# Decay product in two 32-row waves, the removal key summed in PSUM, 512-column products in halves, and the bonus product in front of the scores

## The chip, the cores and the metric

The kernel runs on one core of one Trainium2 chip. The metric is the device time of one execution in microseconds (us). Five engines work side by side, each through its own instruction list in order, and wait for one another through semaphores: TensorE (PE in the profile, with its weight loads as PEld), VectorE (DVE), ScalarE (ACT), GpSimd (POOL) and SyncE (SP, here only for issuing DMAs).

## What is computed

A block of a language model in float32: a recurrent attention layer over 8 sequences of 512 steps and 256 channels in 16 heads, then a mixture-of-experts layer. Only the attention layer's projections matter here; cut to these, the reference reads:

```python
xrg, xwa, xk, xv = x[None] + xx[None] * (lo + time_maa)
k = xk @ Wk.T
w2 = jnp.tanh(xwa @ decay_w1.T) @ decay_w2            # 64 hidden rows
w = -jax.nn.softplus(-(time_decay + w2)) - 0.5
kk = k + jnp.tanh(xk @ kkk_w1.T) @ kkk_w2             # 16 hidden rows
kk = kk / norm(kk per head)
a = sigmoid(time_aaaaa + xwa @ aaa_w1.T @ aaa_w2)
ma = sigmoid(time_misc_a + xwa @ ma_w1.T @ ma_w2)
k = k * ma + k * a * (1.0 - ma)
mk = sigmoid(time_misc_k + xk @ mk_w1.T @ mk_w2)
k = k * exp(w * mk);  b = -kk * a;  decay = exp(-exp(w))
# then per step: s = s*decay + (s a) b + v k, y = s r
rk = (r * k * time_faaaa).sum(-1)                     # the "bonus" per head
y = (group_norm(y) * ln_w + ln_b + rk * v) * g @ Wo.T
```

## The kernel before

**Blocks and bodies.** The 512 steps are cut into 16 blocks of 32 steps; a block has 8 x 32 = 256 columns (`COLS`), and the 256 channels lie in two halves of 128 partitions, so a whole tensor of a block is 128 x 512. A software pipeline runs over bodies n = -2 to 18. Body n makes the projections and scores of block n+1, turns keys and values of block n, solves, reads out and updates the state of block n-1, and projects, normalizes and stores block n-2, with the router's product of block n-3. The order inside a body is written out by hand for each engine in the functions `body(n)`. The mixture-of-experts layer follows after the last body and isn't touched.

**Banks.** Six PSUM banks are handed from job to job in a fixed order, the `Ring`. "z@1" is the job z in bank 1. A job's first product waits (`wait_empty`) until the steps listed for the bank's previous job in `freed` are done, and readers wait (`wait_full`) for its last product.

**The stretch in question on PE.** `hidden` makes the hidden rows (64 of the decay, then 16 each of four others, at the starts 64, 80, 96, 112). `square(.., "k", ..)` makes k in bank 3. `decay_a_kk` makes z (the decay's exponent) as one product over all 128 rows, then a and kk side by side, each over 32 rows; `ma_mk` makes ma and mk side by side. `router` (block n-3, 8 columns each) and `project_out` (block n-2) follow, then the first half of `solve`, `norms` (head sums of kk squared), the second half of `solve`, the products r and v with transposes of keys and values, `read_out`, `bonus`, `update`, `read_out`, and the `scores`.

**ACT and DVE.** ACT copies k out of its bank (`keep_k`, L1085), turns z into its biased copy and its sigmoid (`keep_z`, `sigma_of_z`, L1058), and applies the other sigmoids; the helper line of all biased halves is L1029. DVE adds kk and k (`sum_kk`, L1420), scans the decay (`sum_decays`, L1400, which waits for the sigmoid of z), forms the key gains (L1406, L1408), adds the tokens of block n-2 (`add_tokens`, L1546, which waits for `project_out`), and goes on to the masked keys (`mask_removal` L1476, `mask_keys` L1445) that `scores` waits for. Each fp32 product is two records in the trace. L576 is the line of the helper `fill`, L622 that of `from_hidden`, L718 `solve`, L662 `scores`, L594 `low_2` (the mixing of the next block but one), L1389 the first reader of `low_2` on DVE.

## Time and profile before

| | |
|---|---|
| median of 3 runs | 1076.15 us (1071.28 to 1077.69) |
| the profiled execution's own time | 1076.19 us |
| its span, first to last instruction | 1074.1 us |
| PE busy | 980.1 us (91%) |
| DVE busy | 768.0 us (71%) |
| ACT busy | 519.9 us (48%) |
| mean granted clock of PE, share of full speed | 0.951 |
| bodies with blocks in all stages | 39.2 to 46.9 us each |

PE's busy share is high, but PE is no proof of a bound by itself: its records overlap the waits of the others, and a body ends where the last of PE, DVE and ACT lets the next one go on. The granted clock has two levels, 1.0 (2.4 GHz) and 0.5 (1.2 GHz); a body whose mean is under 1.0 holds a stretch at the lower one.

### The profile page before, as it was taken

The numbers are of one execution on the slowest core, as the hardware profiler recorded it, in microseconds if no ns is written. First come the engines' busy times: TensorE is split into PE (matmuls) and PEld (weight loads), VectorE is DVE, ScalarE is ACT, GpSimd is POOL, SyncE is SP. The second block draws the span as 40 slices with busy tenths as digits, with TensorE's granted clock in tenths as the row PEclk, the third lists the DMA queues.
The fourth block names the chain that finished last, engine by engine and source line by source line (L and its number), as shares of the span: only waits on it lengthen the run. The fifth ranks groups of instructions, "written<-read, shape, count | busy, mean of one in ns | idle before, by whom it ended". The sixth has DMA issues, their size and how long they took to land.

```text
span 1074.1 us, 42156 instructions
## 1 busy us (share of the span) xinstructions
PE 980.1 (91%) x16652; PEld 801.8 (75%) x16653; DVE 768.0 (71%) x1793; ACT 519.9 (48%) x1081; POOL 613.1 (57%) x1135
## 2 busy tenths in 40 slices
PE   8898989999999989999999998679899999999995
PEld 5676777777777767777777776557899898989894
DVE  5766788889879778887688885266476666666663
ACT  4474576677677576676476783221122121212120
POOL 1088786788886787785867876810133333333321
PEclk9997999999999999998799998689999999999998
DMA  5113225225324225224143133746545445544430
GB/s 121 40 21 81 71 33 110 65 51 111 77 47 101 70 44 111 72 42 107 17 101 87 28 91 85 206 115 232 217 163 176 161 174 162 176 158 170 158 119 4
DMA packets 208894, 112.14 MB, mean 104 GB/s; under 512 B 172508, under 2 KB 192224, under 8 KB 208352
## 3 DMA queue, kind: packets, MB, share of 16 engines
q1 hardware_dynamic: 202352, 100.92, 35.0%
q0 software_dynamic: 3744, 8.40, 2.3%
q8 instruction: 121, 1.98, 0.8%
q10 hardware_dynamic: 2640, 0.54, 0.3%
q14 instruction: 37, 0.30, 0.1%
HBM read 85.57 MB, written 26.08 MB: 104 GB/s over the span
## 4 chain that ended last, share of the span: by engine, by line
PE 61%; DVE 14%; issue 8%; POOL 6%; DMA 5%; ACT 4%; DVEq 1%; SPq 1%; ACTq 0%; POOLq 0%
PE bank L576 16%; PE bank L970 12%; PE bank L983 9%; PE bank L662 6%; PE ry L983 4%; PE bank L718 3%; POOL arena L1914 3%; POOL arena L1911 3%; DVE bank L1389 2%; PE ry L692 2%; PE bank L594 1%; PE bank L622 1%; PE bank L950 1%; PE ry L698 1%; PE bank L740 1%
## 5 line engine op out<-in xcount | busy, mean ns | idle before, releaser
L576 PE MATMUL bank<-arena 128*128 128x256 f32 (+2 forms) x992 | 280.9, 422 | 22.4 <-DVE arena L1434 9.5
L1914 POOL TENSOR_TENSOR arena<-arena 128x30 f32<-128x30 f32 (+14 forms) x480 | 261.6, 545 | 37.6
L1911 POOL TENSOR_TENSOR arena<-arena 128x30 f32<-128x30 f32 (+14 forms) x480 | 250.5, 522 | 36.4
L576 PEld LDWEIGHTS bank<-arena 128*128 128x128 f32 x992 | 178.5, 203 | 67.9 <-issue 31.5
L970 PEld LDWEIGHTS bank<-arena 128*128 128x128 f32 x1248 | 146.8, 194 | 5.8 <-issue 3.0
L970 PE MATMUL bank<-arena 128*128 128x128 f32 x1248 | 147.5, 277 | 3.1 <-DVE arena L1820 2.5
L1498 DVE TENSOR_TENSOR arena<-bank,arena 128x512 f32<-128x512 f32 x128 | 79.5, 684 | 53.1 <-PE bank L662 53.1
L1302 ACT ACTIVATE arena<-arena 128x1 f32<-128x1 f32 x39 | 11.5, 294 | 178.6 <-DVE arena L1774 178.6
L983 PE MATMUL bank<-arena 128*128 x416 | 96.4, 385 | 0.1
L1945 POOL COPY arena<-arena 128x1 int32 (+1 forms) x39 | 7.1, 183 | 146.4 <-DVE arena L1838 146.4
L983 PEld LDWEIGHTS bank<-arena 128*128 128x128 f32 x416 | 76.9, 190 | 14.5 <-issue 4.9
L662 PE MATMUL bank<-arena 32*128 32x64 f32 x2048 | 68.9, 276 | 10.6 <-issue 6.4
L1939 POOL DMA_INDIRECT arena<-scr_x,arena x39 | 41.2, 1056 | 62.4 <-DVE arena L1756 31.4
L662 PEld LDWEIGHTS bank<-arena 32*128 32x128 f32 x2048 | 64.0, 189 | 14.9 <-issue 13.4
L1389 DVE SCALAR_TENSOR_TENSOR bank<-bank,arena 128x256 f32<-128x256 f32 x128 | 56.1, 484 | 22.2 <-PE bank L594 22.2
L670 PE MATMUL bank<-arena 128*128 128x128 f32 x432 | 62.5, 279 | 4.2 <-DVE arena L1511 1.6
L670 PEld LDWEIGHTS bank<-arena 128*128 128x128 f32 x432 | 52.1, 144 | 18.8 <-issue 12.4
L1904 POOL MEMSET arena<- 128x32 f32 x16 | 2.5, 157 | 111.2 <-DMA arena<-scr_n 111.2
L718 PEld LDWEIGHTS bank<-arena 32*64 32x64 f32 x2048 | 40.1, 157 | 34.6 <-issue 29.6
L1820 DVE TENSOR_SCALAR arena<-bank,arena 128x128 f32<-128x128 f32 x156 | 43.9, 345 | 24.6 <-issue 19.9
L1947 POOL DMA_INDIRECT out_dram<-arena x39 | 39.8, 1021 | 34.9 <-DVE arena L1804 20.8
L718 PE MATMUL bank<-arena 32*64 32x32 f32 x2048 | 43.8, 239 | 15.1 <-DMA arena<-scr_u 13.9
(173 smaller groups left out, 1757.7 us busy)
## 6 DMA issues: line engine op xcount, KB each, us to landing
arena<-in_W SPq DMA_DIRECT2D x47, 1024.0 KB, 5.1
scr_n<-arena SPq DMA_DIRECT2D x64, 128.0 KB, 3.0
arena<-scr_n SPq DMA_DIRECT2D x16, 512.0 KB, 3.7
scr_u<-arena SPq DMA_DIRECT2D x16, 512.0 KB, 4.5
arena<-scr_u SPq DMA_DIRECT2D x62, 128.0 KB, 2.9
arena<-in_xTp SPq DMA_DIRECT2D x32, 132.0 KB, 4.0
arena<-in_x SPq DMA_DIRECT2D x64, 64.0 KB, 2.7
scr_x<-arena SPq DMA_DIRECT2D x64, 64.0 KB, 1.8
```

What stands on the lines that cost most here:

```text
L576: mm = pe.matmul(ring.tile(m, name)[0:rows, to], lhsT, rhs, start=(i == 0), stop=(i == len(terms) - 1))
L662: mm = pe.matmul(ring.tile(m, f"sc{f}{p}")[:, b * 2 * TB:(b + 1) * 2 * TB], bkm[r, f * B + b, :], aq[m % 2][r, f * B + b].rearrange("p x t ...
L670: mm = pe.transpose(ring.tile(m, name)[:, i * P:(i + 1) * P], src, ident)
L718: mm[bank] = pe.matmul(ring.tile(m, f"x{bank}")[x_rows_of(e), at:at + 32], Ux[m % 2][r, g % 4, g // 4, e].rearrange("p h t -> p (h t)"), R ...
L970: mm = pe.matmul(hidT_ps[t // 4][:, (t % 4) * P:(t % 4 + 1) * P], W1[s][:, k, t * P:(t + 1) * P], xnT[:, k, :], start=(k == 0), stop=(k == ...
L983: mm = pe.matmul(y_ps[s][:, 0:D], hidT[s][:, t, :], W2f[:, bass.ds(e * (FT * D) + t * D, D)], start=(t == 0), stop=(t == FT - 1))
L1389: xm_ok.inc(m, f"{g}{h}", STT(out=part, in0=part, scalar=prm(f"maa{g}", h), in1=dx[:, h], op0=ALU.add, op1=ALU.mult))
L1498: score.inc(m, name, TT(sc[m % 2][:, f, p].rearrange("p k e x t -> p (k e) (x t)"), ring.tile(m, name)[:, :].rearrange("p (b n) -> p b n", ...
L1820: relu_dve.inc(str(t), nc.vector.tensor_scalar(hidT[s][:, t], hidT_ps[1][:, (t - 4) * P:(t - 3) * P], b1f[:, bass.ds(e * FT + t, 1)], 0.0, ...
L1911: inv_ok.inc(f"m{s}", TT(t, U[:, 0:s, s:s + 1].broadcast_to(shape), U[:, s:s + 1, s + 1:TB].broadcast_to(shape), ALU.mult))
L1914: inv_ok.inc(f"a{s}", TT(U[:, 0:s, s + 1:TB], U[:, 0:s, s + 1:TB], t, ALU.add))
L1939: nc.gpsimd.indirect_dma_start(out=xg[:, s], out_offset=None, in_=x_rows, in_offset=bass.IndirectOffsetOnAxis(ap=index, axis=0), bounds_ch ...
```

## The change

Five edits, all in the 16 bodies that have a block n+1 to project.

1. `decay_a_kk` now makes in one wave of three products, side by side, the first 32 hidden rows of z, all of a, and the 32 rows of kk; kk is added onto the product k that is still in bank 3, as the first product there starts the bank and the others don't. The wave waits for all three banks first; the bank of kk is free when `keep_k` has read it.
2. `decay_ma_mk` is a second wave with the other 32 rows of z, and ma and mk; z is complete after it. It stands behind `router`, and `logit` moves from bank 3 to bank 0.
3. DVE's `sum_kk` is gone. ACT copies the sum out of the bank instead (`keep_kk`) and squares it from the bank; ACT's order becomes a, logits, copy and square of kk, z.
4. `norms`, `centre_y` and `variance_y` each make two products of 256 columns instead of one of 512.
5. `bonus` moves behind the second `read_out`.

```diff
-        proj: "k z0 z1 sg a0 a1 ma0 ma1 abs sq sab mk0 mk1 ..."
-        comb: "kk scan t f k2 ..."
+        proj: "k a0 a1 kk sq z0 z1 sg ma0 ma1 abs sab mk0 mk1 ..."
+        comb: "scan t f k2 ..."
-        freed: "kk": [(comb, "kk")]
+        freed: "kk": [(proj, "sq")]
-        ... (1,"z@1 a@5 kk@3 ma@4 mk@2"), (-3,"logit@3"), (-2,"wo@0"), ...
+        ... (1,"a@5 kk@3"), (-3,"logit@0"), (1,"z@1 ma@4 mk@2"), (-2,"wo@0"), ...
             def decay_a_kk(m):
                 hid_act.wait(pe, m, "decay", "copy", "kkk")
-                from_hidden(m, [[("z", 2, slice(0, P), hid)]])
-                from_hidden(m, [[("a", 0, slice(64, 96), hid), ("kk", 0, slice(96, 128), kkh)]])
+                for name in ("z", "a", "kk"):
+                    ring.wait_empty(pe, m, name)
+                for h, to in both:
+                    mm_z = pe.matmul(ring.tile(m, "z")[:, to], w_out[0:32, 2, hs(h)], hid[0:32, :], start=(h == 0), stop=False,
+                                     skip_group_check=True)
+                    mm_a = pe.matmul(ring.tile(m, "a")[:, to], w_out[64:96, 0, hs(h)], hid[64:96, :], start=True, stop=True)
+                    mm_kk = pe.matmul(ring.tile(m, "kk")[:, to], w_out[96:128, 0, hs(h)], kkh[96:128, :], start=False, stop=True,
+                                      skip_group_check=True)
+                mm_z.then_inc(half_decay, 1)
...
+            def decay_ma_mk(m):
+                pe.wait_ge(half_decay, m + 1)
+                for name in ("ma", "mk"):
+                    ring.wait_empty(pe, m, name)
+                for h, to in both:
+                    mm_z = ... w_out[32:64, 2, hs(h)], hid[32:64, :], start=False, stop=True
+                    mm_ma, mm_mk = ... as before
             def norms(m):
-                fill(m, "ss", [(all_cols, [(head_sum, flat(nrm))])])
+                fill(m, "ss", [(to, [(head_sum, nrm[:, h])]) for h, to in both])
...
 PE body(n):
                 if has(n + 1):
-                    ma_mk(n + 1)
-                if -1 <= n <= 0:
-                    keep_busy(4, ry_bank[0])
-                if has(n - 3):
                     router(n - 3)
+                    decay_ma_mk(n + 1)
+                    keep_busy(4, ry_bank[0])   # n = -1, 0
...
-                    bonus(n + 1)               # between the two read_outs
+                    bonus(n + 1)               # behind the second
 ACT body(n):
-                    keep_z sigma_of_z keep_a keep_ma abs_of_z keep_logits(n - 3) square_kk sigma_of_abs keep_mk
+                    keep_a keep_logits(n - 3) keep_kk square_kk keep_z sigma_of_z keep_ma abs_of_z sigma_of_abs keep_mk
 DVE body(n):
-                    sum_kk(n + 1)
```

PE's list around the decay product, in a body that has all stages; the lines of the changed kernel are shifted, L622 becomes L621, L623, L624 (z, a, kk) and L635, L637, L638 (z, ma, mk), and L576 becomes L577. Before:

```order
L576 MATMUL bank<-arena 128x256 x6
L670 MATMUL bank<-arena 128x128 x4
L622 MATMUL bank<-arena 128x256 x10
L576 MATMUL bank<-arena 128x8 x4
L576 MATMUL bank<-arena 128x256 x4
L718 MATMUL bank<-arena 64x32 x32
L576 MATMUL bank<-arena 128x512
L718 MATMUL bank<-arena 64x32 x32
```

and now, from the second half of the first wave on:

```order
L621 MATMUL bank<-arena 128x256
L623 MATMUL bank<-arena 128x256
L624 MATMUL bank<-arena 128x256
L577 MATMUL bank<-arena 128x8 x4
L635 MATMUL bank<-arena 128x256
L637 MATMUL bank<-arena 128x256
L638 MATMUL bank<-arena 128x256
L635 MATMUL bank<-arena 128x256
L637 MATMUL bank<-arena 128x256
L638 MATMUL bank<-arena 128x256
L577 MATMUL bank<-arena 128x256 x4
L727 MATMUL bank<-arena 64x32 x32
```

The router's four products now stand between the two waves, and the last product of z behind them.

ACT's list over the same stretch, each with the semaphores that it waits for (proj, comb and the filled banks). Before, L1085 is the copy of k, L1150 the copy of turned keys, L1058 the sigmoid of z, L1212 the logits, L1097 the square:

```order
L1085 ACTIVATE arena<-bank 128x512 [waits filled3,comb]
L1150 ACTIVATE arena<-bank 128x512 [waits filled2,filled0]
L1029 ACTIVATE arena<-bank,arena 128x256 [waits filled1,comb]
L1029 ACTIVATE arena<-bank,arena 128x256
L1058 ACTIVATE bank<-arena 128x512 [waits proj]
L1029 ACTIVATE arena<-bank,arena 128x256 [waits filled5,comb]
L1029 ACTIVATE arena<-bank,arena 128x256
L1029 ACTIVATE bank<-bank,arena 128x256 [waits filled4]
L1029 ACTIVATE bank<-bank,arena 128x256
L1064 ACTIVATE arena<-arena 128x512 [waits proj,comb]
L1212 ACTIVATE arena<-bank 128x16 [waits filled3]
L1097 ACTIVATE arena<-arena 128x512 [waits comb,filled0]
```

and now, L1094 being the copy of k, L1226 the logits, L1111 and L1105 the copy and the square of kk, and L1067 the sigmoid of z:

```order
L1094 ACTIVATE arena<-bank 128x512 [waits filled3,comb]
L1164 ACTIVATE arena<-bank 128x512 [waits filled2,filled0]
L1038 ACTIVATE arena<-bank,arena 128x256 [waits filled5,comb]
L1038 ACTIVATE arena<-bank,arena 128x256
L1226 ACTIVATE arena<-bank 128x16 [waits filled0]
L1111 ACTIVATE arena<-bank 128x512 [waits filled3,comb]
L1105 ACTIVATE arena<-bank 128x512 [waits filled0]
L1038 ACTIVATE arena<-bank,arena 128x256 [waits filled1,comb]
L1038 ACTIVATE arena<-bank,arena 128x256
L1067 ACTIVATE bank<-arena 128x512 [waits proj]
L1038 ACTIVATE bank<-bank,arena 128x256 [waits filled4]
```

Five instructions now stand between the copy of the turned keys and the first reader of z, where there was none.

PE's list in front of the scores, before (L752 `read_out`, L740 `update`, L662 `scores`):

```order
L670 MATMUL bank<-arena 128x128 x12
L752 MATMUL ry<-arena 32x32 x32
L576 MATMUL bank<-arena 128x256 x2
L740 MATMUL bank<-arena 32x32 x32
L752 MATMUL ry<-arena 32x32 x32
L662 MATMUL bank<-arena 128x64 x32
```

and now:

```order
L679 MATMUL bank<-arena 128x128 x12
L761 MATMUL ry<-arena 32x32 x32
L749 MATMUL bank<-arena 32x32 x32
L761 MATMUL ry<-arena 32x32 x32
L577 MATMUL bank<-arena 128x256 x2
L671 MATMUL bank<-arena 128x64 x32
```

The bonus (the 128x256 x2) has moved past one `update` and one `read_out`.

## Rows read from the trace of the kernel before

**Rows 1.** The page: span, busy time by engine, granted clock in 40 slices

```profile
span 1074.1 us, 42156 instructions
...
PE 980.1 (91%) x16652; PEld 801.8 (75%) x16653; DVE 768.0 (71%) x1793; ACT 519.9 (48%) x1081; POOL 613.1 (57%) x1135
...
PEclk9997999999999999998799998689999999999998
```

**Rows 2.** Busy time by body, cut where DVE starts L1420

```profile
core 0: us, PE busy (x) PEld busy (x) DVE busy (x) ACT busy (x) POOL busy (x), PEclk, DMA share, GB/s
139.54:178.72 39.18, 35.13 (x899) 27.36 (x900) 33.41 (x62) 27.14 (x50) 29.39 (x56) 1.00 0.26 56
...
296.95:337.41 40.46, 38.02 (x912) 29.82 (x910) 33.67 (x63) 28.34 (x54) 29.36 (x56) 0.96 0.31 70
...
461.42:503.17 41.75, 38.22 (x910) 29.97 (x910) 33.57 (x63) 27.82 (x54) 29.09 (x55) 0.96 0.27 57
503.17:550.11 46.94, 44.72 (x914) 34.56 (x910) 33.71 (x63) 28.74 (x55) 33.85 (x66) 0.82 0.34 71
...
590.78:630.53 39.75, 36.68 (x914) 28.86 (x912) 32.37 (x59) 28.06 (x54) 32.89 (x64) 1.00 0.34 78
```

**Rows 3.** Who PE waited for, 110 to 630 us: us in total, times, longest

```profile
PE bank L576 <- DVE arena L1434: 7.4, 11, 1.2
PE bank L576 <- DVE arena L1420: 5.9, 9, 0.9
```

**Rows 4.** Who DVE waited for, 110 to 630 us

```profile
DVE bank L1389 <- PE bank L594: 16.3, 13, 3.0
DVE arena L1546 <- PE bank L576: 12.9, 11, 2.8
```

**Rows 5.** Timeline of PE, decay product to solve: start, us, line, count

```profile
334.59 2.96 PE L622 MATMUL bank<-arena 128*128 128x256 f32 x20
338.23 2.86 PE L576 MATMUL bank<-arena 128*128 128x8 f32 x16 [0.69 <-DVE arena L1420]
341.02 1.13 PE L718 MATMUL bank<-arena 32*64 32x32 f32 x64
```

**Rows 6.** Timeline of DVE over the same stretch

```profile
337.41 0.68 DVE L1420 TENSOR_TENSOR arena<-bank,arena 128x512 f32<-128x512 f32 x1
338.01 1.20 DVE L1400 TENSOR_TENSOR_SCAN arena<-arena,bank 128x512 f32<-128x512 f32 x1
...
339.83 0.70 DVE L1408 TENSOR_TENSOR bank<-bank,arena 128x512 f32<-128x512 f32 x1
341.20 0.69 DVE L1546 TENSOR_TENSOR arena<-bank,arena 128x512 f32<-128x512 f32 x1 [0.67 <-PE bank L576]
```

**Rows 7.** Timeline of ACT over the same stretch

```profile
334.41 0.60 ACT L1085 ACTIVATE arena<-bank 128x512 f32<-128x512 f32 x1 [0.95 <-PE bank L576]
...
335.72 0.84 ACT L1029 ACTIVATE arena<-bank,arena 128x256 f32<-128x256 f32 x2 [0.22 <-PE bank L622]
336.59 0.60 ACT L1058 ACTIVATE bank<-arena 128x512 f32<-128x512 f32 x1
...
339.30 0.18 ACT L1212 ACTIVATE arena<-bank 128x16 f32<-128x16 f32 x1
```

**Rows 8.** Timelines of PE and DVE in front of the scores

```profile
351.17 1.10 PE L576 MATMUL bank<-arena 128*128 128x256 f32 x4 [0.80 <-DVE arena L1434]
...
352.13 1.75 DVE L1445 TENSOR_TENSOR arena<-arena 128x512 f32<-128x512 f32 x2
...
354.03 0.73 PE L662 MATMUL bank<-arena 32*128 32x64 f32 x17
```

**Rows 9.** Timeline of PE: one product of 512 columns

```profile
322.79 1.12 PE L576 MATMUL bank<-arena 128*128 128x512 f32 x2
```

**Rows 10.** Busy time in two neighbouring stretches, columns as in Rows 2

```profile
313.70:316.80 3.10, 2.57 (x65) 2.39 (x66) 0.71 (x3) 1.34 (x2) 2.79 (x5) 1.00 0.00 0
316.80:320.20 3.40, 3.40 (x16) 2.22 (x19) 2.33 (x4) 0.94 (x3) 2.93 (x7) 0.50 0.02 5
```

More of the change, by code:

```diff
@@ L570, in _, with fill @@
         def _(pe):
-            def fill(m, name, parts, cols=slice(0, HALF * COLS), rows=P):
+            def fill(m, name, parts, cols=slice(0, HALF * COLS), rows=P, started_once=False):
                 ring.wait_empty(pe, m, name)
-                for to, terms in parts:
+                for j, (to, terms) in enumerate(parts):
                     for i, (lhsT, rhs) in enumerate(terms):
-                        mm = pe.matmul(ring.tile(m, name)[0:rows, to], lhsT, rhs, start=(i == 0), stop=(i == len(terms) - 1))
+                        mm = pe.matmul(ring.tile(m, name)[0:rows, to], lhsT, rhs, start=(i == 0 and not (started_once and j)),
+                                       stop=(i == len(terms) - 1), skip_group_check=started_once)
                 ring.fill(m, name, mm)
@@ L612, in hidden @@
                 ring.fill(m, "h", mm)
-            def from_hidden(m, parts):
-                for group in parts:
-                    for name, w, rows, x in group:
-                        ring.wait_empty(pe, m, name)
-                for group in parts:
-                    for h, to in both:
-                        for name, w, rows, x in group:
-                            mm = pe.matmul(ring.tile(m, name)[:, to], w_out[rows, w, hs(h)], x[rows, :], start=True, stop=True)
-                            if h == HALF - 1:
-                                ring.fill(m, name, mm)
@@ L637, in square @@
                 xm_ok.wait(pe, m, f"x{x}")
-                fill(m, name, [(to, [(w_sq[:, w, k, hs(h)], xm[x][:, k]) for k in range(HALF)]) for h, to in both])
+                fill(m, name, [(to, [(w_sq[:, w, k, hs(h)], xm[x][:, k]) for k in range(HALF)]) for h, to in both],
+                     started_once=(name == "k"))
             def gate_1(m):
@@ L880, in body @@
                     read_out(n - 1, 1 if n - 1 < last else 0)
+                if has(n + 1):
+                    bonus(n + 1)
+                if n == 0:
+                    keep_busy(7, ry_bank[0])
                 if n == last + 1:
@@ L1095, in square_kk, with keep_kk @@
                     ring.wait_full(act, m - 1, "ss")
-                comb.wait(act, m, "kk")
-                proj.inc(m, "sq", A(flat(nrm), flat(kk), ACT.Square))
+                proj.inc(m, "sq", A(flat(nrm), bank(m, "kk"), ACT.Square))
+            def keep_kk(m):
+                if m:
+                    comb.wait(act, m - 1, "kkn")
+                ring.wait_full(act, m, "kk")
+                proj.inc(m, "kk", A(flat(kk), bank(m, "kk"), ACT.Copy))
             def keep_gate(m):
@@ L1415, in key_exponent @@
                                      op0=ALU.add, op1=ALU.mult))
-            def sum_kk(m):
-                ring.wait_full(dve, m, "kk")
-                proj.wait(dve, m, "k")
-                comb.inc(m, "kk", TT(flat(kk), ring.tile(m, "kk")[:, :], flat(kt), ALU.add))
             def gain_keys(m):
-                comb.wait(dve, m, "f", "kk")
+                comb.wait(dve, m, "f")
                 comb.inc(m, "k2", TT(flat(kt), flat(kt), ring.tile(m, "ma")[:, :], ALU.mult))
@@ L1642, in body @@
                     mix_stage(n + 2)
-                if has(n + 1):
-                    sum_kk(n + 1)
                 if n == last + 2:
```

40 lines of the change are left out of this document (24 added, 16 removed), and 2 rows, old and new, of the table ring.

## The prediction

> **What bounds the kernel now.** The page comes first: PE has a record running 91% of the span [rows 1], so a change on PE looks worth its full size. Then the windows by body, to see what a body costs and what moves it. The chains of waits of PE and DVE follow, and last the timelines of one body, to see who waits for whom in what order. The fourteen bodies between 139 and 631 us cut at DVE's L1420 tell two things: the clean ones at granted clock 1.00 take 39.2 to 39.75 us (five of them), those with one stretch at half clock 40.5 to 41.9 (six), one with more 46.9 [rows 2]. A slow stretch so costs about 41.15 - 39.4 = 1.8 us (mean of the six against mean of the clean).
>
> The loop that closes a body runs through both engines in turn. DVE waits for PE's `low_2`: 16.3 us in 13 waits [rows 4]. From then on DVE works through its list to the masked keys (L1445), and PE starts the scores 0.15 us behind their end, 354.03 against 352.13 + 1.75 = 353.88 [rows 8]. Then PE alone leads, through scores, state read-out and the next `low_2`. In DVE's part one wait of note is left, that for `project_out`, 0.67 us in this body, 12.9 us in 11 waits in all [rows 4, 6]. So whatever comes before the scores counts only as far as it moves DVE's list; PE's own 0.7 to 0.8 us waits there [rows 5, 8] are slack, not price.
>
> **The decay in two waves.** On PE, the old group has twelve rounds one behind the other (four for z, four for a and kk together, four for ma and mk together: each product is two records) in 2.96 us with its drain [rows 5], some 0.24 us a round. The new one has eight, which saves about 0.96 us of PE, and the 0.69 us wait of the router goes too, since its bank no longer hangs on `sum_kk`. But the result z comes later, and this is what DVE needs.
> - The first wave waits for all three banks, kk's being free when the copy of k ends: 334.41 + 0.60 = 335.01 [rows 7]. The old z had started at 334.59 [rows 5]. So start at about 335.08, that is 0.5 us lost, with nothing beside it on PE.
> - A wave of four rounds takes 0.95 us to the next instruction and 1.13 us to its reader on ACT (334.59 to 335.72, [rows 5, 7]). The first is handed over at 336.2, the router starts at 336.0.
> - The router: from 338.23 to the solve at 341.02 are 2.79 us, of which eight records of 256 columns take 8 x 0.23 = 1.84, so it takes 0.95 [rows 5]. The second wave then runs from 337.0, and z is complete for ACT at 338.1.
> - ACT meanwhile does a (336.2 to 337.05), the logits (0.18) when the router is through at 337.15, the copy and the square of kk (0.60 each, as the copy of k, which overlap by 0.1), to about 338.4 [rows 7]. The copy and sigmoid of z took from 335.72 to 337.19 = 1.47 us [rows 7]. Starting at 338.3 they end at 339.8.
> - DVE's scan waits for that sigmoid. It started at 338.01 with no wait, because `sum_kk` (0.68) lay in front of it [rows 6]. Now it starts at 339.8: 1.8 us later, though DVE has one instruction less. The 0.6 us that DVE gains by that is spent waiting.
> - Behind it, L1546 would come at 341.20 + 1.8 without its old wait of 0.67 [rows 6]: **1.1 us later**. `project_out` is through by 340.1 (337.95 + 1.84 and its drain), so it no longer covers anything. DVE has no other wait to absorb 1.1 us before the keys, so the scores start 1.1 us later, and this goes round in every body.
>
> PE's other steps don't turn this. `solve` takes bank 1 after z, so it waits for the scan's end (339.8 + 1.2 = 341.0, where it stood before); `norms` takes bank 0 after `project_out`, so it waits for L1546's end, 343.0. PE idles some 0.5 + 1.1 + 1.0 there; the saved 0.96 us is spent in these waits. ACT's further steps move by as much as the scan, up to 1.8 us at most, and DVE meets the logarithm that it needs (L1412) about when it is ready.
>
> **Over the run.** Six bodies like the one shown: 6 x 1.1 = 6.6. The first full one, where L1546 had no wait: 1.8. Of the 12.9 us of waits for `project_out` [rows 4], 12.9 - 6 x 0.67 = 8.9 are left for five more bodies; four in which PE was slow exactly there have 1.7 to 2.8 each (longest in [rows 4]), which could swallow all of 1.8, so 0 to 1.1 each, taken at the middle, 2.2. The last two have what is left of it, some 0.4 each: 2 x 1.4 = 2.8. The first three have no tokens to add and nothing to cover z: 5.4, and two of them have two filler products between the waves, 0.8 each: 1.6. Sum 20.4 us, with a clock as before.
>
> **The clock.** The granted clock was 0.50 from 316.8 to 320.2, behind a stretch of small 32-row products and waits in which PE was busy 2.57 of 3.10 us at clock 1.00 [rows 10]. The change makes another such place: waits of 0.5, 1.1 and 1.0 us around 32-row waves, the router and the half solves, between about 334.6 and 343. Two of the five clean bodies falling to half clock there would cost 2 x 1.8 = 3.6. Bounds: no slow stretch at all in the bodies, 7 x 1.8 + 5.8 = -18 us; one in every clean body and a second in some of the others, +15. I take +3.6, near the rows' own frequency. The Trainium skill, TensorE: Matmul & The Clock Gate (Part 1, HAM oscillation), lays the fall to idle gaps between bursts and asks to keep PE busy. By that rule alone the waits of about 1 us would cost nothing here and the sum stays at 20.4; rows 10 show a fall behind a stretch without one long gap, so I don't rely on it.
>
> **The halves.** A product of 512 columns took 1.12 us, two of 256 took 1.10 [rows 8, 9]. So nothing; the bounds are -0.1 and +0.1 us for each of three, and only `centre_y` lies where PE leads, so at most 16 x 0.1 = 1.6 us either way. The Trainium skill speaks against this edit: in the same page, Part 3 (What overlaps and what doesn't), a weight load overlaps with a running product only when their row groups differ. By that, the two more loads of 128 rows in each pair would lie open, and at the page's figure of 128 columns in some 0.11 us a load that would be an estimated 3 x 2 x 0.11 = 0.6 us a body on PE. The equal 1.12 and 1.10 us contradict it, and the sum goes by them.
>
> **The bonus.** Its wait for L1434 (7.4 us in 11 waits [rows 3]) goes, 0.80 us in this body. But `update` and `read_out` behind it then run earlier up to a wait of the same length for the keys, which end 353.88 whether PE waits once or twice [rows 8]. The product itself, 1.1 us, fits in that wait: PE comes to the bonus about 1.1 us behind its old pace, near 352.9, and to the scores at 353.95, while the keys are ready at 355.0. Price 0; were that cover gone, nothing would be added either, since the product ran before the scores already.
>
> **Rivals.**
> - *PE is the bound, and the change takes 0.96 off it* (faster). For it speaks the 91% [rows 1] and the waits for `project_out` [rows 4]. It needs z to reach DVE by 337.4; then `sum_kk` (0.6) and L1546's wait (0.67) go, 1.27 us in some 12 bodies: 1076.2 - 15 = **1061 us**. Against it the place of the second wave.
> - *The clock holds up better*: the dense bonus right before the scores ends the slow stretches behind them, about five in the bodies, so 20.4 - 5 x 1.8 = 11 us: **1087 us**.
> - *The waits hide z everywhere*: PE is late in most bodies as in the four with 1.7 to 2.8 us of cover, so half of the 20.4 goes or more: **1083 us**.
> - *The clock falls in every body* (slower still): the new waits are followed by half clock from `project_out` on, PE comes late to the scores as well: 20.4 + 15: **1112 us**.
>
> **How the numbers follow.** The profiled execution took 1076.19 us, the median is 1076.15, so its sum stands for both: 1076.2 + 20.4 + 3.6 = 1100.2, or **1100 us**. Chances: this forecast 0.44, the worse clock 0.20, the better clock 0.14, the hidden z 0.12, PE as the bound 0.10. The range leaves out the fastest rival and the far end of the worse clock: 1080 to 1116. About 1% (10.8 us) is what a measurement of this kernel can tell from no change. Slower by over 1% (above 1087): 0.44 + 0.20 + about half of the two middle rivals = 0.76. Within 1%: 0.14. Faster: 0.10.
>
> **What would show it.** Right: in the profile after, DVE sits idle some 2 us in front of the scan with ACT's sigmoid of z as the releaser, and no longer in front of L1546; PE waits for the scan before the solve and for the keys before the scores; clean bodies take 40.4 to 40.8 us; the two-wave group takes about 1.9 us in all; the halves take 1.1 us. Wrong: a scan that starts as soon as DVE is there, or clean bodies under 39.2 us, would say that z is not late; bodies over 41.5 with clocks of 0.9 and less that the clock, not the wait, sets the time.

## The result, and the profile after

The changed kernel takes 1122.56 us (median of 4 runs, 1117.18 to 1126.95), against 1076.92 before: a ratio of 1.044, 95% interval 1.038 to 1.049. Six more runs beside a later experiment gave 1121.29 us and 1.043 (1.038 to 1.049). The direction was forecast, the size (1100) was not: the time lies over the range. The ratios here leave out, on both sides, runs over 1.5% above a kernel's fastest; the medians are of all runs.

The page of the profiled execution (1119.93 us), lines as in [rows 1]:

```profile
span 1117.9 us, 42460 instructions
...
PE 987.2 (88%) x16812; PEld 826.9 (74%) x16813; DVE 757.5 (68%) x1777; ACT 530.0 (47%) x1097; POOL 611.1 (55%) x1135
...
PEclk9998989899988899799998898777999999999998
```

The busy times hardly changed: DVE 10 us less, ACT 10 us more, PE 7 us more (a record made at half clock takes longer, so PE's busy time rises with it). So the 44 us are waits and clock. Busy time in three stretches, cut at the scans of blocks 3 and 15, with the same cut of the kernel before behind it:

```profile
core 0: us, PE busy (x) PEld busy (x) DVE busy (x) ACT busy (x) POOL busy (x), PEclk, DMA share, GB/s
0.00:140.71 140.71, 118.03 (x1828) 92.39 (x1829) 91.02 (x166) 79.48 (x142) 74.76 (x144) 0.96 0.33 70
140.71:673.65 532.94, 470.75 (x11040) 381.33 (x11040) 395.98 (x717) 346.52 (x649) 384.09 (x731) 0.92 0.31 67
673.65:1117.90 444.25, 398.46 (x3946) 353.15 (x3944) 270.54 (x895) 104.05 (x308) 152.24 (x262) 0.94 0.46 151
```

```profile
140.15:631.13 490.98, 455.15 (x10909) 355.56 (x10907) 403.96 (x730) 337.36 (x633) 386.14 (x732) 0.96 0.34 73
```

Twelve full bodies hold 532.94 - 490.98 = 42.0 of the 43.8 us; the head has +0.6, the tail +1.3. Half-clock time in them, from the mean PEclk as 2 x (1 - clock) x time, rose from about 38 to 85 us. It isn't so much that the clock fell more often, 12 times instead of 8, as that it stayed down longer: seven of the eight stretches of before lasted 3.4 us and one 13.7, ten of the twelve after lasted 6.8 to 10.2. One of them began 1.1 us behind the end of the wait in front of the norms, which is the second line here:

```profile
275.06 1.13 PE L727 MATMUL bank<-arena 32*64 32x32 f32 x64 [1.01 <-DVE arena L1416]
277.05 1.10 PE L577 MATMUL bank<-arena 128*128 128x256 f32 x4 [0.86 <-DVE arena L1557]
```

```profile
278.18:285.01 6.83, 6.83 (x78) 5.86 (x79) 5.53 (x11) 3.00 (x7) 6.12 (x10) 0.50 0.01 2
```

Two of the twelve bodies ran at 1.00, and some were far from it (compare [rows 2]):

```profile
232.01:273.78 41.77, 36.20 (x921) 29.43 (x920) 33.10 (x60) 28.83 (x55) 31.37 (x60) 1.00 0.35 74
501.01:542.23 41.22, 36.11 (x922) 29.30 (x920) 32.84 (x61) 28.94 (x55) 29.52 (x56) 1.00 0.34 69
315.76:364.22 48.46, 42.10 (x922) 34.12 (x920) 33.06 (x61) 28.89 (x55) 32.78 (x63) 0.86 0.29 64
451.44:501.01 49.57, 43.70 (x922) 35.36 (x920) 33.43 (x60) 28.82 (x55) 35.71 (x69) 0.83 0.32 69
```

I cut every body of both traces at the same instructions, by the starts and ends of the instructions (mean us; clean means clock 1.00 throughout, in brackets how many bodies):

| part of the loop | before, clean (5) | after, clean (2) | before, all 12 | after, all 12 |
|---|---|---|---|---|
| scan to end of masked keys (DVE) | 15.94 | 14.97 | 16.68 | 16.17 |
| masked keys to scores (PE starts) | 0.32 | 0.84 | 0.50 | 1.87 |
| scores to next `low_2` (PE) | 10.60 | 10.97 | 11.05 | 11.31 |
| `low_2` to the copy of k | 9.25 | 9.11 | 9.27 | 9.44 |
| start of the copy of k to end of z's sigmoid | 2.78 | 5.49 | 2.78 | 5.51 |
| sigmoid to scan | 0.54 | 0.10 | 0.63 | 0.10 |
| body | 39.43 | 41.49 | 40.92 | 44.41 |

The two clean bodies are 2.06 us longer than those of before, where 40.4 to 40.8 us in all were forecast. The timelines of ACT just in front of a clean body's first scan, and of DVE in that body, answer to [rows 6, 7]; the sigmoid of z is L1067, the scan L1416, the tokens L1557:

```profile
226.21 0.60 ACT L1094 ACTIVATE arena<-bank 128x512 f32<-128x512 f32 x1 [0.97 <-PE bank L577]
...
228.19 0.84 ACT L1038 ACTIVATE arena<-bank,arena 128x256 f32<-128x256 f32 x2 [0.89 <-PE bank L623]
229.12 0.18 ACT L1226 ACTIVATE arena<-bank 128x16 f32<-128x16 f32 x1
229.47 0.60 ACT L1111 ACTIVATE arena<-bank 128x512 f32<-128x512 f32 x1 [0.16 <-issue]
...
230.44 0.84 ACT L1038 ACTIVATE arena<-bank,arena 128x256 f32<-128x256 f32 x2
231.31 0.60 ACT L1067 ACTIVATE bank<-arena 128x512 f32<-128x512 f32 x1
```

```profile
232.01 1.22 DVE L1416 TENSOR_TENSOR_SCAN arena<-arena,bank 128x512 f32<-128x512 f32 x1 [4.08 <-ACT bank L1067]
...
234.46 0.68 DVE L1557 TENSOR_TENSOR arena<-bank,arena 128x512 f32<-128x512 f32 x1
...
244.05 1.28 DVE L1487 TENSOR_TENSOR arena<-bank,arena 128x512 f32<-128x512 f32 x2
245.25 1.73 DVE L1456 TENSOR_TENSOR arena<-arena 128x512 f32<-128x512 f32 x2
```

z's sigmoid ends 5.7 us behind the start of k's copy here (5.49 or 5.50 in the other eleven), and DVE waits for it in every body; the wait in front of the tokens is gone. That was forecast. PE in the same body:

```profile
233.29 1.14 PE L727 MATMUL bank<-arena 32*64 32x32 f32 x64 [1.21 <-DVE arena L1416]
235.28 1.10 PE L577 MATMUL bank<-arena 128*128 128x256 f32 x4 [0.86 <-DVE arena L1557]
...
242.78 0.76 PE L761 MATMUL ry<-arena 128*32 128x32 f32 x64
245.48 0.76 PE L749 MATMUL bank<-arena 128*32 128x32 f32 x64 [1.94 <-DVE arena L1487]
246.08 0.76 PE L761 MATMUL ry<-arena 128*32 128x32 f32 x64
246.76 1.13 PE L577 MATMUL bank<-arena 128*128 128x256 f32 x4
247.82 2.01 PE L671 MATMUL bank<-arena 32*128 32x64 f32 x64
```

The two waves take 1.06 and 1.07 us in front of this body, 2.1 in all where 1.9 were forecast. The waits in front of the solve and of the norms are those forecast too (1.1 and 1.0). The third was not: `update` (L749) waits 1.94 us for L1487, the masked removal keys. Bank 0 goes from the squared norms, which L1487 reads last, to the state update (`freed["ss"]` names the step bm1). PE has 13.8 us of this wait in the twelve bodies. Behind it now stand the update, a read-out and the bonus, and only then the scores: they start at 247.82, 0.84 us after the masked keys are done (245.25 + 1.73 = 246.98). In the kernel before, the bonus ran before that wait and the gap was 0.15 us [rows 8].

### The profile page after: what moved, and what is told of

Its sections match the earlier page's. It is cut to its first block, busy times and chain, and to the rows that moved or that the text cites. A ratio compares the mean times of both kernels' runs of the same rounds, so it can differ in the third digit from the quotient of the medians.

```text
span 1117.9 us, 42460 instructions
## 1 busy us (share of the span) xinstructions
PE 987.2 (88%) x16812; PEld 826.9 (74%) x16813; DVE 757.5 (68%) x1777; ACT 530.0 (47%) x1097; POOL 611.1 (55%) x1135
## 4 chain that ended last, share of the span: by engine, by line
PE 63%; DVE 11%; issue 8%; ACT 6%; POOL 6%; DMA 5%; SPq 1%; DVEq 1%; ACTq 0%; POOLq 0%
PE bank L577 17%; PE bank L979 11%; PE bank L992 9%; PE bank L671 6%; PE ry L992 4%; POOL arena L1923 3%; POOL arena L1920 3%; PE bank L727 3%; PE ry L701 2%; PE bank L679 2%; PE ry L707 2%; PE bank L749 1%; PE bank L596 1%; PE bank L612 1%; PE bank L959 1%
## 5 line engine op out<-in xcount | busy, mean ns | idle before, releaser
L577 PE MATMUL bank<-arena 128*128 128x256 f32 (+1 forms) x1088 | 294.8, 413 | 17.3 <-DVE arena L1557 9.7
L577 PEld LDWEIGHTS bank<-arena 128*128 128x128 f32 x1088 | 206.7, 210 | 70.0 <-issue 30.2
L979 PEld LDWEIGHTS bank<-arena 128*128 128x128 f32 x1248 | 145.3, 192 | 5.6 <-issue 2.9
L992 PEld LDWEIGHTS bank<-arena 128*128 128x128 f32 x416 | 77.1, 190 | 14.3 <-issue 4.9
L671 PEld LDWEIGHTS bank<-arena 32*128 32x128 f32 x2048 | 67.2, 199 | 15.9 <-issue 14.0
L671 PE MATMUL bank<-arena 32*128 32x64 f32 x2048 | 72.2, 287 | 7.3 <-issue 3.5
L727 PEld LDWEIGHTS bank<-arena 32*64 32x64 f32 x2048 | 43.9, 170 | 44.7 <-issue 18.8
L727 PE MATMUL bank<-arena 32*64 32x32 f32 x2048 | 47.8, 250 | 31.5 <-DMA arena<-scr_u 17.4
L679 PEld LDWEIGHTS bank<-arena 128*128 128x128 f32 x432 | 53.8, 147 | 14.5 <-issue 7.2
L1956 POOL DMA_INDIRECT out_dram<-arena x39 | 39.7, 1018 | 34.9 <-DVE arena L1813 20.8
L1829 DVE TENSOR_SCALAR arena<-bank,arena 128x128 f32<-128x128 f32 x156 | 43.9, 345 | 21.8 <-issue 18.1
```

Of the source, the lines that this page charges most:

```text
L577: mm = pe.matmul(ring.tile(m, name)[0:rows, to], lhsT, rhs, start=(i == 0 and not (started_once and j)), stop=(i == len(terms) - 1), skip_ ...
L671: mm = pe.matmul(ring.tile(m, f"sc{f}{p}")[:, b * 2 * TB:(b + 1) * 2 * TB], bkm[r, f * B + b, :], aq[m % 2][r, f * B + b].rearrange("p x t ...
L679: mm = pe.transpose(ring.tile(m, name)[:, i * P:(i + 1) * P], src, ident)
L727: mm[bank] = pe.matmul(ring.tile(m, f"x{bank}")[x_rows_of(e), at:at + 32], Ux[m % 2][r, g % 4, g // 4, e].rearrange("p h t -> p (h t)"), R ...
L979: mm = pe.matmul(hidT_ps[t // 4][:, (t % 4) * P:(t % 4 + 1) * P], W1[s][:, k, t * P:(t + 1) * P], xnT[:, k, :], start=(k == 0), stop=(k == ...
L992: mm = pe.matmul(y_ps[s][:, 0:D], hidT[s][:, t, :], W2f[:, bass.ds(e * (FT * D) + t * D, D)], start=(t == 0), stop=(t == FT - 1))
```

## The experiments

All ratios are against the kernel before, measured beside it on the same chip. "Bodies" is the time of the same twelve bodies in one profiled execution, with the half-clock time in them. These two vary from execution to execution of one program (the two of the changed kernel differ by 7 us), and some of the profiled executions are far from their kernel's median: `u_zearly` is 13 us above it, `b_kksum` 13, `b_halves` 12, `b_repeat` 7 and `u_repeat` 5 us below; the others are within 4.

| kernel | median us (runs) | ratio, 95% interval | bodies us | half clock us |
|---|---|---|---|---|
| before, beside each group of runs | 1073 to 1078 | | 491 | 38 |
| changed | 1122.6 (4), 1121.3 (6) | 1.044 (1.038-1.049), 1.043 (1.038-1.049) | 533, 526 | 85, 85 |
| `u_bonus` | 1109.8 (4) | 1.031 (1.022-1.039) | 524 | 82 |
| `u_whole`, `_again`, `_third` | 1112.3 (4), 1111.4 (6), 1111.9 (6) | 1.027 (1.018-1.036), 1.032 (1.024-1.039), 1.034 (1.030-1.039) | 526, 525, 529 | 104, 82, 96 |
| `u_zdense` | 1097.0 (4) | 1.018 (1.007-1.028) | 519 | 61 |
| `u_zdense_bonus` | 1090.9 (4) | 1.014 (1.005-1.023) | 507 | 41 |
| `u_zdense_bonus_whole` | 1086.3 (4) | 1.012 (1.004-1.021) | 503 | 44 |
| `u_repeat` | 1109.7 (4) | 1.038 (1.030-1.046) | 517 | 34 |
| `u_zearly` | 1141.7 (4) | 1.058 (1.049-1.066) | 565 | 150 |
| `u_zearly_repeat` | 1152.1 (4) | 1.075 (1.065-1.085) | 557 | 82 |
| `u_zearly2` | 1112.6 (4) | 1.036 (1.027-1.044) | 524 | 65 |
| `u_zearly2_bonus` | 1101.0 (4) | 1.024 (1.014-1.034) | 510 | 55 |
| `b_bonus` | 1090.7 (10) | 1.005 (0.998-1.011) | 511 | 68 |
| `b_halves` | 1078.8 (12) | 1.003 (0.998-1.007) | 487 | 31 |
| `b_z64` | 1077.2 (10) | 1.005 (1.002-1.009) | 495 | 48 |
| `b_kksum` | 1092.7 (4) | 1.023 (1.013-1.033) | 494 | 38 |
| `b_repeat` | 1081.7 (10) | 1.004 (0.999-1.008) | 493 | 27 |

**The bonus, put back in the changed kernel (`u_bonus`) and moved alone (`b_bonus`).**

```diff
-                if has(n - 1) and n - 1 < last:
-                    update(n - 1, 0)
-                if has(n - 1):
-                    read_out(n - 1, 1 if n - 1 < last else 0)
                 if has(n + 1):
                     bonus(n + 1)
+                if has(n - 1) and n - 1 < last:
+                    update(n - 1, 0)
+                if has(n - 1):
+                    read_out(n - 1, 1 if n - 1 < last else 0)
```

> The changed kernel with the bonus product back between the two read-outs. Theory A (the bonus costs): behind the change the state update waits for the end of the masked removal keys (bank 0 is theirs before it), and now the bonus of 1.1 us comes between that and the scores, so the scores start 0.84 us behind the masked keys in clean bodies where it was 0.1. Undone, this gap falls back to 0.1 to 0.3 us and the kernel takes 12 x 0.7 = 8 us less, 1114 us, or down to 1100 if the slow stretches around it go too. Theory B (my prediction's step, the bonus is free): no change, 1122 us within 3. Either way the time from the copy of k to the sigmoid of z stays at 5.5 us.

> The kernel before with only the bonus product moved behind the second read-out. Theory A: the update waits for the removal keys, the scores come 0.7 us later in each of 12 full bodies: 1076 + 8 = 1085 us, more if the clock falls more often. Theory B (the bonus is free): 1076 us within 3.

Put back, a clean body's gap closes. DVE and PE in the kernel `u_bonus`, one such body:

```profile
197.85 1.28 DVE L1487 TENSOR_TENSOR arena<-bank,arena 128x512 f32<-128x512 f32 x2
199.05 1.75 DVE L1456 TENSOR_TENSOR arena<-arena 128x512 f32<-128x512 f32 x2
```

```profile
198.08 1.10 PE L577 MATMUL bank<-arena 128*128 128x256 f32 x4 [0.60 <-DVE arena L1445]
199.28 0.75 PE L749 MATMUL bank<-arena 128*32 128x32 f32 x64
199.92 0.92 PE L761 MATMUL ry<-arena 128*32 128x32 f32 x64
200.97 1.29 PE L671 MATMUL bank<-arena 32*128 32x64 f32 x37
```

The scores start 0.17 us behind the keys, the bonus fills what would be the wait, and the kernel gains about 12 us by the medians. Over all twelve bodies the gap is still 1.34 us (1.87 and 1.74 in two traces of the changed kernel): in nine of the eleven bodies that aren't clean, PE comes 1.1 to 2.5 us late even so. Moved alone in the kernel before, the wait appears and the gap grows to 0.9 to 1.0 us in the four clean bodies. The median of the ten runs is 14 us up, and nine of them lie above the highest of the 13 beside them; the ratio rests on the three fastest alone, and its interval spans 1. PE's waits in `b_bonus`, 140 to 651 us:

```profile
PE bank L740 <- DVE arena L1476: 21.0, 11, 2.2
```

So theory A holds by the profiles, in both directions, and by the time in one, where the intervals 1.022 to 1.039 and 1.038 to 1.049 just touch. What it had wrong is where the price lies. The clean bodies of `b_bonus` take 39.65 us, 0.2 more than those of before: the gap is 0.6 us longer in them and the rest of the loop 0.4 us shorter. Most of the 20 us by which its twelve bodies grew lies in the others, with 68 instead of 38 us at half clock.

**The decay product dense again (`u_zdense`), and where the second wave was.** The first wave makes a and kk alone; in the second, z is one product over 128 rows, with ma and mk behind it.

```diff
-                    mm_z = pe.matmul(.. w_out[0:32, 2, hs(h)], hid[0:32, :], start=(h == 0), stop=False, ..)
...
-                    mm_z = pe.matmul(.. w_out[32:64, 2, hs(h)], hid[32:64, :], start=False, stop=True, ..)
+                for h, to in both:
+                    mm_z = pe.matmul(ring.tile(m, "z")[:, to], w_out[:, 2, hs(h)], hid, start=True, stop=True)
```

> The changed kernel with the decay product dense again, as one product over 128 rows, in the place of the second wave (behind the router); a and kk alone in the first. PE works 0.95 us more in each body, z comes no earlier (5.5 us). Theory C (rows that no longer work let the clock fall): the half-clock time in the 12 full bodies falls from 85 us to under 60 and the kernel is faster, 1105 to 1115 us, though it does more on PE. Rival (the new waits of PE let it fall, not the missing rows): half-clock time within 15 us of 85 and 1118 to 1128 us.

This is the largest single share: the median is 25 us less (three runs at 1095 to 1098, one at 1113), with 0.7 us more of PE work in a clean body (36.9 against 36.2). z comes no earlier (5.4 to 5.7 us in most bodies), PE's wait for the removal keys stays (20.4 us in 12 waits), and its two clean bodies take 41.0 and 41.2 us, near the 41.5 of the changed kernel. So little of the gain lies on the path of a clean body. Half-clock time fell from 85 to 61 us, just over the 60 expected, and the time fell further than expected. But one wait of PE did go: that for the scan in front of the solve, 11.8 us in 11 waits over the whole changed kernel, is 0.8 us in 2 here, since PE is still busy with the products ahead of it. Whether the clock held up by that or by the rows, this run can't tell. Its bodies, by the same cut:

```profile
140.11:659.23 519.12, 470.58 (x10991) 376.61 (x10990) 397.43 (x717) 346.68 (x649) 385.50 (x732) 0.94 0.32 69
```

**Rows without time (`b_z64`).** In the kernel before, `slice(0, P)` of z becomes `slice(0, 64)`, whose other rows are zero anyway.

> The kernel before with the decay product over its 64 real hidden rows instead of 128 (the other rows of its weights are zero, so the values are the same). Nothing changes in the order, in the waits or in how long a product streams. Theory C (the clock goes by how much of the array works, rows included, and the dense decay product held it up): every gap at full clock as before, from the copy of k to the sigmoid of z 2.8 us, but more half-clock time in the 12 full bodies than the 38 us of before, 50 us or more, and 1080 to 1095 us. Theory Z (only waits and order count): 1076 us within 4.

It is 0.5% slower: 1.005, interval 1.002 to 1.009, half clock 48 against 38 us in the profile. But the sigmoid of z also came 0.19 us later (2.97 against 2.78), which I had not expected and can't explain; 12 x 0.19 = 2.3 us of the 4 may be that. The time lies where theory Z had it (1076 within 4), the half-clock time between the two. So this run doesn't show an effect of rows on the clock.

**Dense work put into the waits (`u_repeat`, `b_repeat`).** In the changed kernel, two products of `project_out` are made twice and the last four transposes of the values four times; in the kernel before only these transposes are repeated, three times in all.

```diff
-                               for j in range(NTILE_BLK)])
+                               for j in (0, 1, 1)])
-                for i, src in enumerate(sources):
+                for i, src in [pair for _ in range(times) for pair in enumerate(sources)]:   # times = 4 or 3
```

> The changed kernel with dense products repeated in PE's waits: two of the output projection's four products are made twice (0.86 us, in front of the solve, where PE waits 1.2 us for the scan), and the last four transposes of the values four times (1.3 us more, in front of the update, where PE waits 1.9 us). The output is the same. Theory C: clean bodies stay at 41.2 to 41.8 us, but the half-clock time in the 12 full bodies falls from 85 us to under 45, and the kernel takes 1105 us or less. Theory Z (waits alone): 1122 us or a little more, since work was only added.

> The kernel before with the last four transposes of the values made three times (0.87 us more of dense work), just in front of the read-out behind which PE waits 0.8 us for the bonus. Same output. Theory C (dense work in a wait buys clock): clean bodies stay at 39.4 us, half-clock time in the 12 full bodies falls from 38 to under 25, 1065 to 1072 us. Rival (the added work shows in full): 12 x 0.9 = 10 us more, 1085 us.

In the changed kernel more work gave less time: 12 us less, and 34 instead of 85 us at half clock.

```profile
143.02:660.33 517.31, 473.97 (x11231) 387.59 (x11230) 398.25 (x718) 346.19 (x649) 386.91 (x736) 0.97 0.32 70
```

Six of the twelve bodies are clean instead of two. The clock is up in every run: 0.953 to 0.962 in the four, against 0.919 to 0.940 in the ten of the changed kernel. The gain in time is less certain, since the ratios 1.038 (1.030 to 1.046) and 1.044 (1.038 to 1.049) overlap; but work was only added, and theory Z left no room for a gain. Together with `u_zdense`, whose interval lies clear below, that makes the clock a cause of its own in the changed kernel. The step isn't free: several bodies had the scores 2 to 3 us behind the keys, so the repeats delay PE where it comes late anyway, and 1105 was missed by 5 us. In the kernel before the same trick gave nothing (1.004, interval 0.999 to 1.008): 27 us at half clock instead of 38 in the profiled execution, but the bodies took 493 us. Over all runs the clock is nearly the same (0.953 on average against 0.951), so a gain in clock isn't shown there.

**An earlier z (`u_zearly`, `u_zearly_repeat`, `u_zearly2`, `u_zearly2_bonus`).** The second wave directly behind the first, the router behind both; ACT takes z right behind a.

```diff
                     keep_a(n + 1)
-                    keep_logits(n - 3)
-                    keep_kk(n + 1); square_kk(n + 1)
                     keep_z(n + 1); sigma_of_z(n + 1)
+                    keep_kk(n + 1); square_kk(n + 1)      # u_zearly: logits behind abs_of_z
+                    keep_logits(n - 3)                     # u_zearly2: here, kk behind abs_of_z
```

> The changed kernel with the second wave directly behind the first, in front of the router, and ACT taking z behind a and before the copy of kk. Theory Z (late z is the main price): from the copy of k to the end of the sigmoid of z 4.5 us instead of 5.5 (2.8 before the change), 1.0 us less in each of 12 full bodies and so 1110 us, less if slow stretches go with the waits. Rival C (the clock decides, whatever the order): the time from k to the sigmoid falls as said, but the half-clock time in the 12 bodies stays about 85 us and the time within 5 us of 1122.

The sigmoid came at 4.59 us as expected, and the kernel lost 19 us more. PE's waits say why, in `u_zearly`, 142 to 706 us:

```profile
PE bank L577 <- ACT arena L1224: 33.3, 11, 3.0
PE bank L749 <- DVE arena L1484: 11.2, 10, 1.6
```

L1224 is the copy of the logits: with `logit` and `wo` in bank 0 one after the other, the output projection waits for ACT, 3 us in a body, behind two 32-row waves and the router. The scan-to-keys part grew from 16 to 21 us and no body ran clean. It was my variant's fault, not a test of the theory.

> The variant with the second wave directly behind the first, which fell to 150 us of half clock in the 12 full bodies, with the same repeated products as above. Theory C: most of the half-clock time goes, below 80 us, and the time falls from 1142 to below 1120; the sigmoid of z stays at 4.6 us behind the copy of k. Against it: the fall begins in the decay waves and the router, ahead of the repeated products, which then only shorten it.

With the dense repeats half clock was 82 us, just over the 80 expected; the 150 it is compared with come from the slowest of four executions, but the clock over the whole run is up in all of them (0.935 to 0.940 against 0.909 to 0.929). The time did not fall at all: 1152 us. Scan to keys still took 18.1 to 20.8 us. So where the wait remains, a better clock gives little back; my forecast of under 1120 was wrong.

> The first variant with an early z had a fault of its own: the output projection takes bank 0 after the logits, and ACT copied the logits only behind kk, so PE waited 33 us for ACT. Here ACT copies them right behind the sigmoid of z. Theory Z (late z is half of the price, the clock the rest): z's sigmoid 4.6 us behind the copy of k instead of 5.5, clean bodies 40.6 to 41.2 us instead of 41.5, half-clock time in the 12 full bodies at or under the 85 us of the changed kernel, 1105 to 1115 us. Rival (two 32-row waves side by side with nothing dense between them pull the clock down whatever follows): half-clock time stays over 120 us and the time over 1125.

> The same with the bonus product back between the read-outs: both delays on the path of a clean body reduced. Theory: clean bodies 39.9 to 40.4 us, scores 0.1 to 0.2 us behind the keys; 1090 to 1100 us. If it still stands over 1110, the clock is what is left.

With the logits copied in time z stays at 4.59 us, and clean bodies take 40.7, 41.2 and 42.0 us. The gain is 9 us by the medians, within overlapping intervals, and 12 more with the bonus back, which agrees with `u_bonus`: the scores come 0.15 us behind the keys in clean bodies. These take 40.2 to 41.5 us, over the 39.9 to 40.4 expected. Moving z 0.9 us earlier does not give 0.9 us a body: scan to keys takes 15.8 us there instead of 15.0, and DVE now waits for L1129, the logarithm on ACT (8.1 us in 11 waits). So ACT, with one more copy, is the next that DVE waits for.

**The addition moved alone (`b_kksum`).** kk summed in PSUM in the kernel before, everything else as it was but for the logits in bank 0.

```diff
-                from_hidden: .. start=True, stop=True
+                from_hidden: .. start=(name != "kk"), stop=True, skip_group_check=(name == "kk")
-                    square_kk(n + 1)                      # ACT
+                    keep_kk(n + 1); square_kk(n + 1)
-                    sum_kk(n + 1)                         # DVE
```

> The kernel before with only kk summed in PSUM: no addition on DVE, ACT copies and squares kk out of its bank behind the logits, the logits in bank 0; the decay product stays one product over 128 rows and first. Both theories: the sigmoid of z still ends 2.8 us behind the copy of k, DVE's list is 0.6 us shorter and PE's wait in front of the router is gone, so a clean body takes 38.7 to 39.0 us instead of 39.4: 1076 - 12 x 0.5 = 1070 us. If the clock falls more often for it (PE then waits in front of the solve instead), up to 1080.

No gain of 6 us: 1.023 (1.013 to 1.033), slower. Clean bodies take 39.4 to 39.6 us, as before, though DVE's list is 0.6 us shorter: DVE waits more for `project_out`, which again waits for the logits.

```profile
PE bank L576 <- ACT arena L1220: 9.6, 11, 0.9
```

```profile
DVE arena L1550 <- PE bank L576: 24.2, 11, 3.0
```

Against 12.9 us before [rows 4]. The run tests the edit together with this queue in bank 0, not alone. Its four runs have clocks of 0.936 to 0.954; the profiled one is the fastest, so where the other 13 us of the median lie isn't shown.

**The halves (`u_whole` three times, `b_halves`).**

```diff
-                fill(m, "ss", [(to, [(head_sum, nrm[:, h])]) for h, to in both])
+                fill(m, "ss", [(all_cols, [(head_sum, flat(nrm))])])
```

and likewise in `centre_y` and `variance_y`; the reverse in `b_halves`.

> The changed kernel with whole products of 512 columns in the norms and in the centring and variance of y. Theory (halves cost nothing, one of 512 takes 1.12 us and two of 256 take 1.10): 1122 us within 3, every gap as in the changed kernel. Rival (the two more weight loads lie open, 0.1 us each, or the half products change the clock): 3 to 10 us either way.

> The changed kernel with whole products once more, in five rounds, since four runs between 1099 and 1121 us settle little. Theory (halves are neutral): 1118 to 1124 us, as the changed kernel. Rival (halves cost): 1109 to 1115 again.

> The kernel before with only the three products of 512 columns made in halves. Theory (halves are neutral): within 3 us of the kernel before, every gap of the full bodies as before. Rival (halves cost, as the 10 us suggest by which the changed kernel with whole products was faster): 1084 us or more, through a lower clock or a later next mixing product.

> The changed kernel itself, beside the next run on the same chip. Halves neutral: the same median as the next run within the spread, 1110 to 1123 us, and then the 1122.6 us of its four first runs were its upper part. Halves cost: 1118 to 1126 us, and the next run 8 us or more below.

> The changed kernel with whole products of 512 columns, beside the run before. Ten runs so far have a median near 1112 us. Halves neutral: within 4 us of the run before. Halves cost: 8 us or more below it.

In the kernel before the halves are neutral (1.003, 0.998 to 1.007). In the changed one they seem not to be: 16 runs with whole products have medians of 1111 to 1112, and beside each other on one chip the changed kernel took 1121.3 and the whole one 1111.9 us, ratios 1.043 (1.038 to 1.049) and 1.034 (1.030 to 1.039). The intervals just touch; I take some 9 us as likely, and most of its place as open. The twelve bodies of the profiled pair don't show it (526 and 529 us); the stretch behind the last scan took 448.5 us in one and 441.1 in the other, but two more traces of whole products have 440 and 445 there and the first of the changed kernel 444. The products themselves take the same time in both forms (1.10 to 1.13 us). One part has a place. Near the end of the attention layer, from DVE's first scan of the routing (L1622) to its last (L1730), all eight traces that have both the halves and the two waves take 26.7 to 28.1 us and the three with whole products 23.7 to 23.8. In these eight, and in none of the other twelve traces, PE pauses there for 1.5 to 2.1 us in a read-out, for no reason that the profile shows. In the changed kernel:

```profile
761.08 0.53 PE L761 MATMUL ry<-arena 128*32 128x32 f32 x19 [1.83 <-issue]
```

The stretch behind it is up to 1.7 us shorter in them, so some 2 to 4 of the 9 us may lie here. It isn't the halves as such: `u_zdense`, `u_zdense_bonus` and `b_halves` have them too, without the pause, and take 23.8 to 25.0 us.

**Do the shares add (`u_zdense_bonus`, `u_zdense_bonus_whole`)?**

> The changed kernel with the dense decay product and the bonus product between the read-outs. If the two shares add, 1097 - 12 = 1085 us; if the clock that the dense product holds up was lost at the bonus, nearer to 1097.

> The same with whole products of 512 columns: what is left of the change is the sum of kk in PSUM and z behind the router. Halves neutral: as the run before within 4 us. Halves cost: some 8 to 10 us less. The late z (5.5 against 2.8 us, of which 0.6 for the addition on DVE and 0.6 for its wait come back) should keep it 8 to 14 us above the kernel before.

Only in part: with the dense product the bonus is worth 6 us instead of 12, the halves 5 instead of 9 (within the spread). Alone the three give 12 + 25 + 10 = 47 us, together 1122 - 1086 = 36. What is left, the late z and the sum in PSUM, costs 1.2% (0.4 to 2.1), some 13 us by the ratio and 8.5 by the medians, within the 8 to 14 expected. Its six clean bodies take 40.5 us, 1.1 more than those of before. None of the versions beats the kernel before.

## Why the prediction was wrong

Two terms of the sum failed: the bonus, priced at 0, and the clock, priced at 3.6 us. The late z was forecast rightly in kind and nearly in size. A third term, the halves at 0, is likely off by some 9 us; its cause stays open.

- **That z comes too late** was right: released by ACT's sigmoid in every body, 5.49 us behind k's copy against 5.39 worked out. The step "1.1 us later at the tokens" is 2.71 - 0.44 (the slack in front of the scan) - 0.97 (the wait for `project_out` and the shorter list behind it) = 1.3 us in clean bodies. Twelve times that is 16 us; the version with only this part and the sum in PSUM left stands 13 us above the kernel before by the ratio, 8.5 by the medians.
- **"The bonus: price 0" failed.** The step said that update and read-out then run earlier, the bonus fits into the wait for the keys, and PE stands at the scores before the keys are ready. It overlooked that `update` itself waits, for the removal keys, through the bank that it takes over, so that update, read-out and bonus all come behind that wait. The trace of before has no such wait, because the bonus covered it: L1476 ended at 352.2, the update started at 352.36. The cover was moved away. Measured: the gap between keys and scores is 0.52 us longer in the clean bodies, 1.4 over all, and undoing it is worth 12 us by the medians. I had asked what hides the bonus, but not what the bonus hides.
- **The clock was right in kind, mis-sized by five times**: "+3.6 us" for it, against (3.50 - 2.06) x 12 = 17 us in the profile (3.50 is what a body grew by over all twelve, 2.06 what a clean one grew by), for 48 us more at half clock, some 0.36 us for each. I had named the place, and it is there: in seven of twelve bodies the clock fell between scan and keys, 2.7 to 4.4 us behind the scan, and in nine of the second trace. What I had wrong is the size of one fall: I took 1.8 us for it from the stretches of before, mostly 3.4 us long, where those of the changed kernel are mostly 6.8 to 10.2. The bound of +15 was near; the likeliest value, by the frequency of before, ignored that the change both adds waits and takes dense work out of the same stretch. `u_zdense` and `u_repeat` show that this is a cause and not a companion.
- **The first bodies**: 7.0 us in the sum, 0.6 measured. Block 0's scan came 2.5 us later (23.93 against 21.47), and the next bodies gave it back: block 2's was 0.4 us later. That this error pulled the other way is luck; without it the miss would have been 29 us instead of 22.
- **The halves**: neutral by the durations and in the kernel before; likely some 9 us in the changed kernel, whose cause stays open beyond the pause shown above. The rule of the Trainium skill that I set aside (TensorE: Matmul & The Clock Gate, Part 3, What overlaps and what doesn't) would have given a price on PE alone, but `b_halves` shows none, and the group of four records took 1.10 to 1.13 us in the changed kernel. The trace speaks against it still.
- **Waits and the clock.** Filling waits of 1 to 2 us with dense products took half clock from 85 to 34 us (`u_repeat`), and the extra product of `u_zdense` runs where PE had waited for the scan; an effect of working rows as such stays unshown. The Trainium skill (TensorE: Matmul & The Clock Gate, Part 1, HAM oscillation) lays the clock's fall to idle gaps, and this agrees with it in kind. It doesn't agree with the reading that waits of about 1 us cost nothing: the fall at 278.18 came behind waits of 1.01 and 0.86 us, and no wait of PE in the lists for these bodies is over 2.2 us.

## What to carry to other kernels

When an operation is moved, list what it covered: look for the next instruction's own wait on a resource that changes hands, even if the trace shows no wait there. Where an engine waits, making its work ahead of the wait cheaper saves nothing and can cost, if its clock falls for it: 0.7 us less of PE work in a body went with 24 us more at half clock in twelve bodies and a kernel 25 us slower. And an instruction's result time counts, not its length: splitting a product to save engine time pays only if its reader doesn't stand behind the second half.

## What was not expected of the hardware

The clock varies between runs of one program, and most of the spread goes with it: the kernel before took 1061.9 us at a mean clock of 0.963 and 1090.9 at 0.936. Over 67 runs of it the slope is 0.37 us for each microsecond at half clock, near the 0.36 above, and the line explains four fifths of the variance. By it, as an estimate, the clock's share of the 45 us is 22: the ten runs of the changed kernel have 162 us at half clock over the whole span on average, the 67 have 103. With kernels like this, differences under 1% need many runs, and the clock of each should be read beside its time.
